# Perceiver decoder on one core: turning the next group's context ahead of the last block, counting weights singly, and moving the wait for the last stores

## The reference, cut to what matters

```
x = x + L0_xattn(layernorm(x), ctx_1024, W_q, W_k, W_v)            # one head
...
x = x + L1_xattn(layernorm(x), ctx_1024, fside, Wq, Wk, Wv, Wo)    # 16 heads of 16, with a bias
...
x = x + L2_xattn(layernorm(x), ctx_1024, Wq, Wk, Wv, Wo)           # 16 heads of 64
...
x = x + L3_xattn(layernorm(x), ctx_1024, mask, Wq, Wk, Wv, Wo)     # 16 heads of 16, masked
```

## Time and profile before

| | us |
|---|---|
| median of 3 runs | 2960.52 (2957.53 to 2962.19) |
| the profiled execution, its own time | 2962.33 |
| its span in the profile | 2960.6 |
| preparation: from the start to the first instruction of the next stage | 757.46 |
| PE busy over the whole span | 2772.9 (94%) |

### The profile page before, as it was taken

How to read it: one execution, slowest core, us unless ns; L and a number is a source line. 1 busy time by engine, 2 the same in 40 slices (tenths; PEclk the granted TensorE clock), 3 DMA queues, 4 the chain that set the end, 5 groups by cost and what they waited for, 6 DMA issues and landing times. The chain is left out here.

```text
span 2960.6 us, 66607 instructions
## 1 busy us (share of the span) xinstructions
PE 2772.9 (94%) x24069; PEld 1854.9 (63%) x24069; DVE 1766.0 (60%) x3578; ACT 1502.4 (51%) x2416; POOL 718.5 (24%) x390
## 2 busy tenths in 40 slices
PE   7999999999898899999999999999999788999989
PEld 5555555555768466666556666666666685666678
DVE  3232332323142777877748888888888618878532
ACT  2333333333341588888336666666666433656521
POOL 2323233232000000000006666666666000000000
PEclk9999999999999799999999999999999798999989
DMA  7887878887834999997622222222222385656455
GB/s 217 290 266 256 250 253 260 250 257 242 268 98 161 419 404 395 395 398 280 234 92 68 65 67 66 63 67 66 67 63 66 104 255 129 158 149 160 116 213 187
DMA packets 331565, 578.28 MB, mean 195 GB/s; under 512 B 79792, under 2 KB 265976, under 8 KB 325752
## 3 DMA queue, kind: packets, MB, share of 16 engines
q1 hardware_dynamic: 331408, 576.06, 59.1%
HBM read 394.96 MB, written 181.04 MB: 195 GB/s over the span
## 5 line engine op out<-in xcount | busy, mean ns | idle before, releaser
L1790 POOL TENSOR_TENSOR l2x_sums<-l2x_sums,all_S 128x768 f32<-128x768 f32 (+1 forms) x195 | 474.0, 2431 | 190.0 <-ACT all_S L2114 184.2
L1994 DVE TENSOR_TENSOR all_S<-all_S,l2x_minus 128x1024 f32<-128x1024 f32 x224 | 382.3, 1707 | 1.9 <-ACT l2x_minus L2110 1.9
L1831 PE MATMUL l2x_key_bank<-ahead_ctx,early_nat_out 128*64 128x512 f32 (+1 forms) x1536 | 323.1, 541 | 0.0
L669 PE MATMUL prep_work<-prep_wv,prep_ctxT 128*128 128x512 f32 x688 | 300.3, 594 | 0.0
L1975 DVE TENSOR_TENSOR l2x_tops<-l2x_scores,l2x_tops 128x768 f32<-128x768 f32 (+1 forms) x208 | 223.4, 1074 | 117.5 <-PE l2x_scores L1847 117.5
L1418 ACT ACTIVATE l3x_pT<-l3x_turned 128x896 f32<-128x896 f32 x224 | 197.6, 916 | 152.6 <-PE l3x_turned L1268 148.1
L2114 ACT ACTIVATE all_S<-all_S 128x1024 f32<-128x1024 f32 x224 | 213.3, 952 | 97.7 <-DVE all_S L1994 97.7
L1167 ACT ACTIVATE all_S<-all_S,l1x_negmax 128x896 f32<-128x896 f32 x224 | 233.1, 1043 | 44.6 <-DVE l1x_negmax L1103 26.3
L1862 PE MATMUL l2x_out<-all_S,l2x_values 128*64 128x128 f32 x3136 | 226.3, 285 | 10.8 <-ACT all_S L2114 10.8
L2102 ACT COPY all_S<-l2x_scores 128x1024 f32<-128x1024 f32 x224 | 201.9, 901 | 65.4 <-PE l2x_out L1862 63.8
L669 PEld LDWEIGHTS prep_work<-prep_wv,prep_ctxT 128*128 128x128 f32 x688 | 129.7, 190 | 162.3 <-issue 152.1
(11 more groups left out here) (688 smaller groups left out, 4692.0 us busy)
## 6 DMA issues: line engine op xcount, KB each, us to landing
l1x_bias<-in_fside_Bx16xSxS_dram SPq DMA_DIRECT2D x112, 896.0 KB, 7.3
scratch_k<-prep_kparts SPq DMA_DIRECT2D x84, 672.0 KB, 3.3
l1x_k_half<-scratch_k SPq DMA_DIRECT2D x32, 1568.0 KB, 9.8
l2x_values<-scratch_v SPq DMA_DIRECT2D x112, 256.0 KB, 2.6
scratch_k<-prep_kparts SPq DMA_DIRECT2D x56, 448.0 KB, 4.8
scratch_v<-prep_st_v SPq DMA_DIRECT2D x11, 2048.0 KB, 9.1
scratch_v<-prep_st_v SPq DMA_DIRECT2D x14, 1536.0 KB, 7.2
l2x_values<-scratch_v SPq DMA_DIRECT2D x112, 192.0 KB, 2.4
```

The costliest lines, as they stand in the source:

```text
L669: last = nc.tensor.matmul(w[:, h, :], ctxT[:, k, j * P:(j + 1) * P], wv2[:, k, h * 512:(h + 1) * 512], start=(k == 0), stop=(k == KT - 1))
L1790: nc.gpsimd.tensor_tensor(sums[odd][:, 0:n], sums[odd][:, 0:n], in_memory(u), ALU.add).then_inc(added, 1)
L1831: last = nc.tensor.matmul(keys_ps[u % 2][half * VW:(half + 1) * VW, 0:n], wk_cur[odd][:, k, :], ahead.piece[u // 2][:, k, c:c + n], start= ...
L1994: nc.vector.tensor_tensor(part, part, minus[:, :].unsqueeze(1).to_broadcast([P, blocks_of(u), P]), ALU.add).then_inc(shifted, 1)
```

## The change

Three things are done.

1. **Turning sooner.** PE's 14 transposes of group g+1 stand ahead of the last block of group g instead of behind it. DVE's and ACT's copies of them into `ctxT` stand ahead of the last block on those engines too (DVE's own emptying of that block comes after them). Of the four copies, the one that overwrites the rows that the last block reads waits for the last block; the others wait for the block before it only. The last block reads rows of bank 3 in a group of 16 blocks, and of bank 1 in a short one. The first block s0 of the next group waits for banks 0 and 1 ahead of its first half, and for all four ahead of its second half.
2. **Weights counted singly.** The two weights needed first (k0 and `wq0`) are loaded first and have a semaphore of their own; each of the others has its own. PE turns k0, makes the query, turns k1 and v1, folds the query, turns k3 and v3. The context of group 0 is loaded ahead of the large weight `wv2`. DVE waits for the biases (`bias_loaded`) at the first key block, and PE waits for `wv2` at the first v2 block.
3. **The last stores.** SP does not wait for them at the end of the preparation. Their semaphores live on, and SP waits for them in the next stage, ahead of value pieces 0, 4, 7 and 8.

The diff, cut to its core:

```diff
-def prepare_context(nc, com, a, scr):
+class ContextStores:
+    def wait_before_chunk(self, sp, c):
+        if c == 0:
+            sp.wait_ge(self.ones, 16)
+            sp.wait_ge(self.fill, 16 * GRP + 16)
+            sp.wait_ge(self.ctxT, 16 * GRP + 16)
+        if c == 4:
+            for s in self.parts:
+                sp.wait_ge(s, 16 * N_COPIES * (2 * GRP + 1))
+        if c == 7:
+            sp.wait_ge(self.narrow, 32 * GRP + 32)
+        if c == 8:
+            sp.wait_ge(self.wide[0], 16 * GRP + 16)
+            sp.wait_ge(self.wide[1], 16 * (GRP - LATE) + 16)
+
+def prepare_context(nc, com, a, scr, stores):
...
+                for t, src in ((nat_w["k0"], a["L0_xattn_W_k"]), (wq0, a["L0_xattn_W_q"])):
+                    sp.dma_start(t[:, :, :], src.rearrange("(k p) n -> p k n", p=P)).then_inc(front_loaded, 16)
+                for n, src in (("k1", a["L1_xattn_Wk"]), ("v1", a["L1_xattn_Wv"]), ("k3", a["L3_xattn_Wk"]),
+                               ("v3", a["L3_xattn_Wv"])):
+                    sp.dma_start(nat_w[n][:, :, :], src.rearrange("(k p) n -> p k n", p=P)).then_inc(rest_loaded[n], 16)
...
+                load(0)
+                sp.dma_start(wv2[:, :, :], a["L2_xattn_Wv"].rearrange("(k p) n -> p k n", p=P)).then_inc(wide_loaded, 16)
                 sp.wait_ge(ones_set, 4)
-                load(0)
...
-                sp.wait_ge(ctxT_stored, 16 * GRP + 16)
-                sp.wait_ge(fill_stored, 16 * GRP + 16)
-                sp.wait_ge(ones_stored, 16)
-                for s in parts_stored:
-                    sp.wait_ge(s, 16 * N_COPIES * (2 * GRP + 1))
-                sp.wait_ge(narrow_stored, 32 * GRP + 32)
-                sp.wait_ge(wide_stored[0], 16 * GRP + 16)
-                sp.wait_ge(wide_stored[1], 16 * (GRP - LATE) + 16)
...
-                pe.wait_ge(weights_loaded, 16 * 6)
+                pe.wait_ge(front_loaded, 16 * 2)
+                turn_weights("k0")
...
+                def group(g, plan):
                     for i, (what, j, _e) in enumerate(plan):
                         w = work[:, i % 2]
+                        if i == len(plan) - 1 and not is_last(g):
+                            turn_group(g + 1)
...
                             for h in range(2):
+                                if what == "s0":
+
+                                    for e in "vs":
+                                        pe.wait_ge(turn_copied[e], g * 2 + 3 + h)
...
                     if t == ts[0]:
 
                         eng.wait_ge(ctxT_stored, g * 16 + 16)
-                        eng.wait_ge(work_full, filled(g))
+                    if not (isinstance(g, int) and g == 0):
+
+                        eng.wait_ge(work_full, filled(g) - (0 if last_block // 2 == t else 1))
...
@@ -930,6 +977,7 @@
         if heads == 1:
             for at in range(GRP // 2):
                 c = j * (GRP // 2) + at
+                before_values(sp, c)
                 sp.dma_start(v_half[j][:, at * GC:(at + 1) * GC, :], v_src(h, c)).then_inc(v_loaded[c], 16)
```

More of the change, by code:

```diff
@@ L419, in vector_end, with __init__ @@
         dve.wait_ge(self.k_step, self.n + self.total)
-def prepare_context(nc, com, a, scr):
+class ContextStores:
+    def __init__(self, ph):
+        self.ctxT, self.fill, self.ones, self.narrow = (
+            ph.sem(s) for s in ("ctxT_stored", "fill_stored", "ones_stored", "narrow_values_stored"))
+        self.parts = [ph.sem(f"parts_stored{i}") for i in range(2)]
+        self.wide = [ph.sem(f"wide_values_stored{i}") for i in range(2)]
+    def wait_before_chunk(self, sp, c):
[12 more added lines that the diff above has]
+def prepare_context(nc, com, a, scr, stores):
     with phase(nc, "prep") as ph:
@@ L505, in each_group, with is_last @@
             one(GRP - 1, plan)
+        def is_last(g):
+            return isinstance(g, int) and g == GRP - 1
         def rank(i):
@@ L621, in _ @@
                 last.then_inc(q0T_in_psum, 1)
+                for n in ("k1", "v1"):
+                    pe.wait_ge(rest_loaded[n], 16)
+                    turn_weights(n)
                 pe.wait_ge(q0T_ready, 1)
-                pe.wait_ge(wT_ready, 5)
+                pe.wait_ge(wT_ready, 1)
                 for e in range(KT):
@@ L628, in _, with turn_group @@
                 last.then_inc(qfT_in_psum, 1)
-                pe.wait_ge(qfT_ready, 1)
-                pe.wait_ge(wide_loaded, 16)
-                def group(g, plan):
+                for n in ("k3", "v3"):
+                    pe.wait_ge(rest_loaded[n], 16)
+                    turn_weights(n)
+                pe.wait_ge(wT_ready, 5)
+                def turn_group(g):
                     pe.wait_ge(ctx_loaded, g * 16 + 16)
@@ L666, in group @@
                         elif what == "v2":
+                            if isinstance(g, int) and g == 0:
+                                pe.wait_ge(wide_loaded, 16)
                             for h in range(2):
@@ L716, in _, with take_weights @@
                 norm_vector(dve)
-                for n_i, n in enumerate(nat_w):
+                def take_weights(n_i, n):
                     dve.wait_ge(wT_in_psum, n_i + 1)
@@ L748, in group @@
                             continue
+                        if i == len(plan) - 1 and not is_last(g):
+                            take_turned(dve, nc.vector.tensor_copy, g + 1, (0, 2), plan)
                         if what in ("v1", "v2", "v3"):
@@ L781, in group @@
                 def group(g, plan):
-                    take_turned(act, nc.scalar.copy, g, (1, 3))
                     nk = 0
                     for i, (what, j, e) in enumerate(plan):
+                        if i == len(plan) - 1 and not is_last(g):
+                            take_turned(act, nc.scalar.copy, g + 1, (1, 3), plan)
                         if e == "s":
@@ L802, in group @@
                             nk += 1
+                take_turned(act, nc.scalar.copy, 0, (1, 3), plan)
                 each_group(act, group)
@@ L3462, in latent_decoder @@
                 embedding = EmbeddingStart(nc, ph, a)
-                l0_cross_attention(nc, com, a, scr, embedding.load)
+                l0_cross_attention(nc, com, a, stores, embedding.load)
                 l0_attention(nc, com, a, embedding, expert0.load)
```

63 lines of the change are left out of this document (32 added, 31 removed).

## The result

| | us |
|---|---|
| after, median of 4 runs | 2939.31 (2938.48 to 2940.94) |
| before, median of 4 runs beside them | 2959.03 (2956.25 to 2962.19) |
| ratio, 95% interval | 0.9933 (0.9921 to 0.9944) |
| span of the profiled execution, before and after | 2960.6 and 2939.2 |

The kernel is 0.67% faster. The forecast was 2939.0 us, and 21.5 us less for the profiled execution; its span fell by 21.4. So the sum is met, in part by luck, as the terms show. Its terms are looked at one by one.

What follows compares the result with a forecast made beforehand. PE was taken to bound the stage, so only its idle time could be won. Terms of 11.5 + 0.9 + 4.0 + 5.1 = 21.5 us off the profiled execution gave 2939.0 us against the median; range 2931 to 2949.

Steps and rivals of the forecast that it cites:

- Loop boundaries, 11.5 us: Ten boundaries between groups 3 and 13: copies under the last block save 1.15 us each, bounds 0 and 1.24.
- Short boundaries, 0.9 us: Boundaries 0 to 3: 0.3 us saved each, ACT's bank 1 copy still waiting; stalls sum set 0, bounds -3 and +2.
- The start, 4.0 us: First group: s0 6.0 us sooner, less 2.0 us of new stall at the second v3 block.
- The end, 5.1 us: Seam to the next stage: without SP's wait for the last stores, products begin 5.1 us sooner.
- If it moves only when the store has landed, at 756.7: Stage's end: first value piece waits for the store, then takes 2.6 us, so products begin at 759.5.
- Claim (c): Loop groups: key stores move 2.7 us towards boundary traffic, hidden by 2.75 us of DMA cover; cost 0, bound 0.5 each.
- the case in which it fails: Key stores late in every group: 0.5 to 1.2 us paid at each loop group's second v3 block, 2949; 12%.
- half a microsecond more: Key stores in the loop: assumed lag from issue to movement, added to 2.2 us of idle DMA as cover.
- The rival of the half clock: Seam of the stages: PE's clock falls in the pause, first products at half speed, 2.5 us lost, 2941.5; 14%.
- Slower: All groups: idle DMA ahead of the key stores is used up, 2.7 us stall at 13 boundaries, 2974; 3%.
- not sooner in effect: PE waits ahead of s0 for ACT as before, or DMAs give both ends back; 2955 to 2960; 3%.

Runs made afterwards that it cites:

- late copies: Changed kernel, but all four copies into ctxT wait for the last block, the transposes still ahead of it; 2947.59 us in a single run.
- whole wait: Changed kernel, but s0 waits for all four banks ahead of its first half; 2944.46 us in a single run.
- weights alone: Kernel before with only the weights counted singly, group turning and last waits as before; 2953.74 us, ratio 0.9987.
- turning alone: Kernel before with only the turning sooner, weights, first loads and last stores' wait as before; 2944.54 us, ratio 0.9953.
- last stores alone: Kernel before with only the last stores' wait moved out of the stage's end; 2956.30 us, ratio 0.9993.
- added loads: Changed kernel plus an unused load per loop group behind the ctxT store, first 512 KB (2940.45 us), then 1024 KB (2965.85 us), one run each.
- first loads: Changed kernel, but group 1's loads and the ctxT store go out ahead of four small parameter loads and the store of ones; 2938.17 us, one run.
- 512 KB more: Changed kernel with one unused 512 KB load behind the store of ctxT in groups 3 to 13; 2940.45 us in one run.
- both: Changed kernel with the last group's v2 store in five pieces, and group 1's loads and ctxT store ahead of the store of ones; 2937.44 us, ratio 0.9927.

## Why the prediction was right, by its own terms

**Loop boundaries, 11.5 us: right.** 1.15 a boundary was forecast, and the period fell from 54.87 to 53.72. The mechanism is shown by the late copies and the whole wait. Of the 1.24 us that were the bound, 0.09 is not seen; it fits the two more waits, but nothing here separates them.

**Short boundaries, 0.9 us: right.** The forecast had 0.9 us left between block and s0; the idle time is 0.84. From group 1 to 2 and 2 to 3 the gain grows by 1.00 and 0.30 us; of the first, 0.77 is the stall of group 1 that is gone. That leaves 0.2 to 0.3 each. The stalls did change place: 1.86 in group 0, none in 1 and 2, 0.59 in 3. In groups 1 to 3 their sum fell from 1.58 (0.77 and 0.81) to 0.59; it had been set at 0.

**The start, 4.0 us: right, with luck in it.** 6.0 less 2.0 was forecast; 5.95 less 1.86 was measured. PE began at 7.51, when `wq0` had landed, and not at 7.0; what came behind made up for it. The stall is the loosest number of the sum. In seven profiles of kernels that are the changed one up to there it was 1.86, 2.34, 1.75, 1.28, 1.09, 1.02 and 0.88, and 0.95 with weights alone; that 2.0 was met is luck of one execution. In the second profile of the changed kernel it was 2.34 and half clock came on top, so that the second s0 came at 61.63 against 64.08 before: 2.45 us, and not 4.

At the last s0 the three terms together are 17.25 us against 16.4 forecast (696.86 - 679.61); in the second profile they are 14.86 (696.86 - 682.00).

**The end, 5.1 us: the mechanism right, the size wrong.** It brought 15.35 - 11.40 = 3.95. The step that failed is the landing of the store ahead of the first value piece. "If it moves only when the store has landed, at 756.7" takes over the 5.7 us that SP had waited for this store in the kernel before, where nothing was queued behind it. By this the products come 759.5 - 751.03 = 8.5 us behind the end of the store's issue; it was 743.38 - 733.78 = 9.6. The store took 7.3 us to land instead of 6.3, with its last part at 175 GB/s, and that is 1.0 of the 1.15 us missing. The piece itself moved as fast as forecast or faster (383 and 370 GB/s in 741 to 743, against 348). The same store lands in 6.3 us in the three kernels where SP waits for it (before, turning alone, weights alone) and in 7.3 in the seven where it is uncut and the value pieces are issued behind it, last stores alone among them. So the loads queued behind it cost the store 1 us; by what means stays open, as do the other 0.15 us. (The prediction also calls this store 2 MB; it is 1536 KB. No number was made from that.)

The rule of the Trainium skill (DMA: Bandwidth & Descriptors, Queues, rings and completion order) that a queue's descriptors are taken in ring order chose 5.1 over 5.7. The trace agrees: up to 740 the packets have the store's size, and from then on the piece's.

**The sum: met by luck to 0.1 us.** The stage came out 0.85 us above its three terms and the end 1.15 under; the two errors nearly cancel. And the stage's own number differs by 2.4 us between the two profiles of the changed kernel.

**Claim (c), DMA "just hidden": right in outcome, wrong in size.** The cover was called 2.75 us for a move of 2.7, and 12% went to the case in which it fails. The added loads show about 0.9 us unused in the changed kernel. The step that was off is the "half a microsecond more" for the lag from issue to movement. Windows of the kernel before:

```profile
433.00:434.00 1.00, 1.00 (x4) 0.49 (x3) 0.00 (x0) 0.88 (x2) 0.09 (x1) 1.00 0.60 242
...
436.00:437.00 1.00, 1.00 (x6) 0.90 (x5) 0.53 (x1) 0.44 (x1) 0.02 (x1) 1.00 0.00 0
437.00:438.00 1.00, 1.00 (x6) 0.87 (x6) 0.00 (x0) 0.50 (x1) 0.42 (x1) 1.00 0.81 297
```

The DMAs were idle from about 433.6 to 437.2, though the store was issued at 436.25: an estimate of 3.6 us of cover from these shares, 0.9 more than the move, which is what the added loads found.

**The rival of the half clock (14%).** Its first half came true: in a pause of 3.83 us the clock fell, 0.2 us before PE resumed at 735.82, and stood at 0.50 until 739. The window behind the fall (the one before it still reads 0.96):

```profile
735.60:735.70 0.10, 0.00 (x0) 0.00 (x0) 0.00 (x0) 0.10 (x3) 0.00 (x0) 0.50 1.01 330
```

Its second half did not, in either of the two profiles of the changed kernel: the clock was back before the products at 743.38, because they waited for the value piece. In three other kernels of this study (last stores alone, first loads, 512 KB more) the first products ran in 4.93 to 4.98 us instead of 3.29, and 1.7 us were lost. There too the clock had been back at full; it fell a second time behind waits for the value piece of 1.88 to 2.33 us, while the changed kernel's, 2.08 and 2.11, had no such fall. So the price came by a wait that the prediction's rival did not have. The Trainium skill (TensorE: Matmul & The Clock Gate, Why this matters for your kernels) warns of a pause between bursts; the fall at the stage's end is seen in every profile, the price only in some, and I would give this rival more than 14% again.

**Slower (3%) and not sooner in effect (3%)** did not come: no loop group stalls, and s0 starts with the block's end.

## What to carry to other kernels

When one engine bounds a stage, look for the work that it waits for at a seam and ask whether the copy, and not the product, can lie under the last block; here moving the transposes alone gave 0.1 us and moving the copies 1.06 more, and most of that needed the consumer to wait by halves. A stage whose DMAs are near their limit can give a saved stall back one or more groups later, so changes to its start should be summed over all its groups, and over more than one profile. To learn how much cover a transfer has, read where it begins to move and not where it is issued, or add traffic in two steps: the first step shows the slack, the second the price. A time to landing read where nothing follows need not hold when loads are queued behind.

## What the runs showed of the hardware that was not expected

- A store of 1536 KB landed in 7.3 us in all eight profiles where loads were issued behind it on the same queue, and in 6.3 in all three where none were. In the changed kernel the rate fell to 218 and 183 GB/s for two microseconds with the DMAs still 0.95 and 0.89 busy, between stretches of over 300; the slow packets were those of the store.
- A stall of about 2 us can cost half clock on top. The changed kernel, in its second profile:

```profile
44.41 4.54 PE L708 MATMUL prep_work<-prep_T_v,prep_ctxT 128*128 128x256 f32 x12 [2.34 <-ACT prep_st_v L748]
```

with windows behind it:

```profile
44.50:45.00 0.50, 0.50 (x3) 0.45 (x4) 0.00 (x0) 0.50 (x1) 0.50 (x1) 0.98 0.00 0
45.00:45.50 0.50, 0.50 (x3) 0.41 (x2) 0.00 (x0) 0.18 (x1) 0.46 (x2) 0.50 0.00 0
...
46.00:48.00 2.00, 2.00 (x6) 1.53 (x6) 0.00 (x0) 0.82 (x1) 1.14 (x1) 0.50 0.90 331
```

  The same 12 matmuls took 2.86 us after 1.86 us of idling in the first profile, and 4.54 here: 1.7 us more. With first loads 1.96 us of idling had the same effect, with "both" 2.25 us had none. So the length of the pause alone did not decide it.
- PE's clock can fall behind the pause, when PE is already working again: in the rows above PE resumed at 44.41, and the clock was full until just before 45.0. At the stage's end of the changed kernel it fell just before PE resumed, and with first loads in 739 to 740 (0.74), when PE had resumed at 738.06.
